# Pair tiles and replicated rows loaded from a DRAM copy of X0, one overlapping transfer each

## What is computed

```python
e = stack([tbl_f[ids[:, f]] for f in range(39)], axis=1)        # (1024, 39, 16)

def cin_layer(X0, Xi, W, b):                                    # H = 128
    Wr = W.reshape(H, 39, Xi.shape[1])
    return einsum('hjk,bjd,bkd->bhd', Wr, X0, Xi) + b[None, :, None]

X0 = e; Xi = X0; res = []
for W, b in ((W0, b0), (W1, b1), (W2, b2)):
    Xi = cin_layer(X0, Xi, W, b)
    res.append(Xi.sum(axis=2))
z = concatenate(res, axis=1)
h = maximum(concatenate([z, dense_ctx], axis=1) @ W_top1 + b_top1, 0)
h = maximum(h @ W_top2 + b_top2, 0)
y = h @ W_top3
```

## Time and profile before

| | us |
|---|---|
| time, median of 3 runs (1387.94 to 1392.07) | 1389.95 |
| the profiled execution's own time | 1388.79 |
| its span | 1386.9 |
| setup, until the first X0 is there | 0 to 56 |
| layer 0 of the first half chunk, TensorE often idle | 56 to 100 |
| one chunk in the steady state (466 to 624) | 158 |
| last MLP steps | 1330 to 1387 |

### The profile page before, as it was taken

How to read it: one execution, slowest core, us unless ns; L and a number is a source line. 1 busy time by engine, 2 the same in 40 slices (tenths; PEclk the granted TensorE clock), 3 DMA queues, 4 the chain that set the end, 5 groups by cost and what they waited for, 6 DMA issues and landing times.

```text
span 1386.9 us, 23238 instructions
## 1 busy us (share of the span) xinstructions
PE 1277.4 (92%) x6029; PEld 1041.8 (75%) x6029; DVE 1082.3 (78%) x2681; ACT 1042.6 (75%) x3356; POOL 893.5 (64%) x663
## 2 busy tenths in 40 slices
PE   3179999999999999999999999999999999999986
PEld 3147777777888787887878777887878788887775
DVE  3068999988877988789877988789877988779940
ACT  2228888878877888788867888688877888688842
POOL 6658676877776687667867597667876266441111
PEclk8559999999999999999999999999999999999998
DMA  6243223413232223303242223313233123310010
GB/s 221 42 115 68 46 72 80 106 30 83 67 97 46 48 63 85 92 21 80 62 108 50 52 63 74 92 33 72 56 90 79 32 68 83 89 32 9 18 39 0
DMA packets 71116, 92.39 MB, mean 67 GB/s; under 512 B 31776, under 2 KB 53792, under 8 KB 69696
## 3 DMA queue, kind: packets, MB, share of 16 engines
q1 hardware_dynamic: 60836, 87.75, 24.4%
q0 software_dynamic: 9984, 2.58, 2.1%
q10 hardware_dynamic: 156, 0.48, 0.1%
HBM read 21.03 MB, written 10.95 MB: 23 GB/s over the span
## 4 chain that ended last, share of the span: by engine, by line
PE 70%; POOL 8%; DVE 7%; issue 6%; DMA 3%; ACT 2%; SPq 2%; ACTq 0%; DVEq 0%; POOLq 0%
PE ring L938 16%; PE ring L940 15%; PE ring L939 15%; PE side L856 5%; POOL e_in L397 4%; PE side L915 4%; PE l_ps L843 4%; PE l_ps L845 3%; PE l_ps L844 3%; DVE terms L785 3%; DVE x_s L741 2%; PE side L871 2%; POOL pairs L429 2%; DMA x_rep<-x_t 2%; POOL pairs_lo L440 2%
## 5 line engine op out<-in xcount | busy, mean ns | idle before, releaser
L626 ACT ACTIVATE terms<-ring,e_both 128x128 f32<-128x128 f32 x2944 | 836.3, 399 | 221.9 <-PE ring L940 219.9
L938 PE MATMUL ring<-w_hi,x_hi 128*128 128x512 f32 (+1 forms) x1280 | 544.8, 426 | 31.4 <-DVE terms L785 27.7
L785 DVE SCALAR_TENSOR_TENSOR terms<-ring,e_both,terms 128x128 f32<-128x128 f32 x1792 | 508.2, 344 | 62.7 <-PE ring L940 58.0
L940 PE MATMUL ring<-w_hi,x_lo 128*128 128x512 f32 (+1 forms) x1280 | 499.7, 390 | 0.0
L939 PE MATMUL ring<-w_lo,x_hi 128*128 128x512 f32 (+1 forms) x1280 | 498.2, 389 | 0.0
L741 DVE TENSOR_REDUCE x_s<-terms 128x32 f32<-128x800 f32 x512 | 488.9, 976 | 0.1
L440 POOL TENSOR_TENSOR pairs_lo<-pairs,pairs_hi 117x1024 fp32r<-117x1024 f32 (+1 forms) x104 | 250.2, 2406 | 191.6 <-ACT pairs_hi L532 190.6
L397 POOL DMA_INDIRECT e_in<-in_tbl,idx x312 | 306.1, 981 | 88.3 <-issue 79.4
L938 PEld LDWEIGHTS ring<-w_hi,x_hi 128*128 128x128 f32 x1280 | 242.8, 190 | 103.0 <-DVE terms L785 42.1
L429 POOL TENSOR_TENSOR pairs<-x_rep,pairs 117x1024 f32<-117x1024 f32 (+1 forms) x104 | 250.3, 2407 | 92.3 <-DMA pairs<-x_t 89.3
L939 PEld LDWEIGHTS ring<-w_lo,x_hi 128*128 128x128 f32 x1280 | 243.4, 190 | 49.2
(11 more groups left out here) (65 smaller groups left out, 610.6 us busy)
## 6 DMA issues: line engine op xcount, KB each, us to landing
pairs<-x_t SPq DMA_DIRECT2D x312, 156.0 KB
x_scratch<-x_s SPq DMA_DIRECT2D x32, 256.0 KB, 2.2
x_r<-x_scratch SPq DMA_DIRECT2D x8, 1024.0 KB, 6.0
x_rep<-x_t SPq DMA_DIRECT2D x45, 156.0 KB
g_t<-in_L_rec_W SPq DMA_DIRECT2D x2, 2496.0 KB, 9.5
e_in<-in_tbl,idx POOLq DMA_INDIRECT x312
x_scratch<-e_both SPq DMA_DIRECT2D x8, 312.0 KB, 7.2
xb<-x_scratch SPq DMA_DIRECT2D x8, 312.0 KB, 3.9
```

The costliest lines, as they stand in the source:

```text
L626: last = nc.scalar.activation(term(d, ACT_BEFORE[d][g] + i), twos(ring[:, (GROUPS * d + g) % RING, i * H:(i + 1) * H]), ACT.Copy, scale=sc ...
L785: nc.vector.scalar_tensor_tensor(out=acc, in0=y, scalar=scale_of(j, d), in1=acc, op0=ALU.mult, op1=ALU.add).then_inc(dve_unit, 1)
L938: nc.tensor.matmul(acc, x1_hi[:, x], w1_hi[:, w], start=True, stop=False)
L940: nc.tensor.matmul(acc, x1_lo[:, x], w1_hi[:, w], start=False, stop=True).then_inc(y_group, 1)
```

## The change

A DRAM tensor `x0t_scratch` of 58 by 2048 is added. A new step on SP's queue, `x0t_write`, copies one half of `x0_t` to it; its semaphore is `x0t_out`. `rep` waits for that copy and loads all 117 rows of `x0_rep` by one transfer whose source has three dimensions: 3 repeats at a step of nothing, 39 rows, 1024 elements. `pair_tile` loads its 117 (or 78) rows by one transfer whose source has 3 (or 2) blocks that begin one row apart and so overlap, 39 rows, 1024 elements. The copy of half 0 stands ahead of `rep`, that of half 1 behind pair tile 1. The first chunk's `rep` moves from ACT's queue to SP's. ACT's evacuation of `x0_t` (line 555) waits for the copies of the chunk before instead of for the loads. Counts on semaphores follow: 16 for each tile instead of 48.

```diff
-                    for n in range(SHIFTS_OF[t]):
-                        s = PER_TILE * t + n
-                        sp.dma_start(products[n * FIELDS:(n + 1) * FIELDS, :],
-                                     x0_t[s:s + FIELDS, half * HALF:(half + 1) * HALF]).then_inc(loaded, 16)
+                    rows = bass.AP(tensor=x0t_dram.tensor, offset=PER_TILE * t * COLS + half * HALF,
+                                   ap=[[COLS, SHIFTS_OF[t]], [COLS, FIELDS], [1, HALF]])
+                    sp.dma_start(products[0:ROWS_OF[t], :], rows).then_inc(loaded, 16)
+
+                def x0t_write(chunk, half):
+                    after(sp, x0t_ready, 4 * chunk + 2 * half + 2)
+                    after(sp, pair_made, PAIR_TILES * (2 * (chunk - 1) + half + 1))
+                    x = slice(half * HALF, (half + 1) * HALF)
+                    sp.dma_start(x0t_dram[:, x], x0_t[:, x]).then_inc(x0t_out, 16)
 
                 def rep(chunk, half):
-                    after(sp, x0t_ready, 4 * chunk + 2 * half + 2)
+                    after(sp, x0t_out, 16 * (2 * chunk + half + 1))
                     after(sp, pair_made, PAIR_TILES * (2 * chunk + half))
-                    for n in range(PER_TILE):
-                        sp.dma_start(x0_rep[n * FIELDS:(n + 1) * FIELDS, :],
-                                     x0_t[0:FIELDS, half * HALF:(half + 1) * HALF]).then_inc(rep_in, 16)
+                    rows = bass.AP(tensor=x0t_dram.tensor, offset=half * HALF,
+                                   ap=[[0, PER_TILE], [COLS, FIELDS], [1, HALF]])
+                    sp.dma_start(x0_rep[:, :], rows).then_inc(rep_in, 16)
...
                 if following:
-                    if layer1:
-                        rep(c + 1, 0)
-                    else:
-                        after(sp, x0t_ready, 2)
+                    x0t_write(c + 1, 0)
+                    rep(c + 1, 0)
                     for i in range(PAIR_TILES):
                         pair_tile(c + 1, i)
+                        if i == X0T_LAST_AFTER:
+                            x0t_write(c + 1, 1)
...
-                            for s in range(2):
-                                if layer1:
-                                    after(act, pair_in[s], loads(c + 1, s))
-                            after(act, rep_in, 16 * PER_TILE * 2 * (c + 1))
+                            after(act, x0t_out, 32 * (c + 1))
...
-                        if following and d == X0T_SLICES[0] + 1:
-                            act.wait_ge(x0t_ready, 2)
-                            for n in range(PER_TILE):
-                                act.dma_start(x0_rep[n * FIELDS:(n + 1) * FIELDS, :],
-                                              x0_t[0:FIELDS, 0:HALF]).then_inc(rep_in, 16)
```

More of the change, by code:

```diff
@@ L32, in build_tower @@
     TILE = [(half, t) for half in range(2) for t in range(PAIR_TILES)]
-    SLOT_BEFORE = [16 * sum(SHIFTS_OF[TILE[k][1]] for k in range(i % 2, i, 2)) for i in range(TILES + 2)]
+    SLOT_BEFORE = [16 * len(range(i % 2, i, 2)) for i in range(TILES + 2)]
     RING = 4
@@ L111, in build_tower @@
     X2_WRITES = {13: 0, 2: 1, 6: 2}
-    X2_LAST_AFTER, X0_AFTER = 9, 11
+    X2_LAST_AFTER, X0_AFTER, X0T_LAST_AFTER = 9, 11, 1
     X2_SLOTS = 8
@@ L185, in pair_slot @@
                 s = i % FIRST_SLOTS
-                count = sum(16 * SHIFTS_OF[k] for k in range(s, i + 1, FIRST_SLOTS))
+                count = 16 * len(range(s, i + 1, FIRST_SLOTS))
                 return pairs[:, s, :] if s < 2 else more_pairs[:, s - 2, :], pair_in[s], count
@@ L189, in pair_slot @@
             return (pairs[:, s, :], pair_in[s],
-                    loads(chunk, s) + SLOT_BEFORE[i] + 16 * SHIFTS_OF[TILE[i][1]])
+                    loads(chunk, s) + SLOT_BEFORE[i] + 16)
         def loads(chunk, s):
-            elsewhere = sum(16 * SHIFTS_OF[i] for i in range(PAIR_TILES) if i % 2 == s and i % FIRST_SLOTS >= 2)
+            elsewhere = 16 * sum(i % 2 == s and i % FIRST_SLOTS >= 2 for i in range(PAIR_TILES))
             return SLOT_BEFORE[TILES + s] * chunk - elsewhere
@@ L198, in build_tower @@
         x0_dram = nc.dram_tensor("x0_scratch", [D, P, FIELDS], f32, kind="Internal").ap()
+        x0t_dram = nc.dram_tensor("x0t_scratch", [WRAPPED, COLS], f32, kind="Internal").ap()
         x2_dram = nc.dram_tensor("x2_scratch", [D, P, H], f32, kind="Internal").ap()
@@ L214, in build_tower @@
         x0t_ps, x0t_ready, x0_out, xb_in = sem("x0t_ps"), sem("x0t_ready"), sem("x0_out"), sem("xb_in")
+        x0t_out = sem("x0t_out")
         rep_in = sem("rep_in")
@@ L392, in _ @@
             sp.wait_ge(x0_out, 16 * CHUNKS)
+            sp.wait_ge(x0t_out, 32 * CHUNKS)
         @block.gpsimd
@@ L426, in multiply_pairs @@
                         pool.wait_ge(pair_made, n)
-                    after(pool, rep_in, 16 * PER_TILE * (2 * chunk + half + 1))
+                    after(pool, rep_in, 16 * (2 * chunk + half + 1))
                     after(pool, loaded, count)
@@ L717, in first_pairs @@
                         if g == made_at:
-                            after(dve, rep_in, 16 * PER_TILE * (2 * chunk + half + 1))
+                            after(dve, rep_in, 16 * (2 * chunk + half + 1))
                             after(dve, loaded, count)
```

## The result

The change makes the kernel slower: median 1572.28 us of 4 runs (1571.42 to 1575.06), against 1389.02 us for the kernel before in runs beside it, a ratio of 1.1315 with a 95% interval of 1.1301 to 1.1329. The forecast was 1549 us, 23 us too little, and inside its range of 1420 to 1690. The profiled execution took 1572.25 us (span 1570.4), 183.5 more than the 1388.79 of before.

A forecast was written before the change was run, and what follows sets the result against it. TensorE, busy 92% of the span, was taken to bound the kernel. 40.3 + 7 x (11.9 + 1.8 + 3.2) = 158.6 us on 1388.79 gave 1547.4, or 1549 us allowing 1.2 to the median; range 1420 to 1690.

The forecast's parts named there:

- the forecast's 7 us: Whole kernel: gain if each coalesced transfer were spread over all DMA engines, giving 1383 us; chance 0.07.
- a busy share of 0.80: Quietest stretch of 39-row loads: read as 13 of 16 DMA engines working, since 13 divides 39.
- copy of 58 rows: Copy of half of `x0_t` to DRAM: two engines, 1.5 us fixed plus 4.7 of data, 6.2 us.
- `x0_rep` and tile 0, one after the other: Two loads after the copy on the same three engines: 8.8 us, then 6.3 more.
- tile 0 late, each chunk: Start of a chunk, seven times: POOL starts at 488.2 instead of 476.31, 11.9 us late with no slack.
- TensorE's waits on ACT, each chunk: TensorE's pauses: 11.9 us at a chunk's start and 3.2 at the change of halves.
- clock, each chunk: Restart after the pause at a chunk's start: 3.6 us at half speed, 1.8 us lost.
- first chunk: Chain of copies and loads without cover: tile 8 at 145.0 instead of 104.71, 40.3 us later.
- The signs that the prediction named: Profile after: first product near 80 us, layer 1 near 140, chunks 175, POOL waiting 18, clock 0.50, DMA share near 3/16.
- The other tiles: Later pair tiles of a half: a load takes 8.8 of the 9.27 us pace, hidden by half a microsecond.
- All wide, 1383: Rival for all transfers: spread in full whatever the outer count, tile 0 2.3 us earlier, 1383 us; chance 0.07.
- Three engines, and slow: Rival for the loads: three engines at 14.4 GB/s make the DMA engine the bound, 1784 us; chance 0.07.

The follow-up runs named there:

- experiment 2: Changed kernel with loads turned to 39 groups of 3 rows, seventh tile padded to 117 rows, copy of 62 rows: 1448.94 us, ratio 1.0428 to the kernel before.
- experiment 5: Changed kernel with one row more in `x0_t` and its copy, 59 instead of 58: 1637.87 us, ratio 1.1777 to the kernel before.
- experiment 3: Changed kernel with loads turned to 39 groups of 3 rows and a copy of 64 rows: 1392.66 us, ratio 1.0031 to the kernel before.
- experiment 4: Changed kernel with each load from DRAM cut into three (two) transfers of 39 rows, copy still 58 rows: 1439.04 us, ratio 1.0358 to the kernel before.

## Why the prediction was right, and by how much it was off

**What decides** was named rightly: a transfer is cut along the outermost counts, three engines for the loads, two for the copies. The trace shows 0.19 (3/16) at 78 GB/s, experiment 2 shows 0.13 (2/16) for a copy of 62 rows, experiment 5 shows 0.06 (1/16), and the steps from 58 to 59 to 64 rows (7.9, 11.8, 3.3 us) are explained neither by size, nor by source, nor by overlap. Single packets agree: the rows of the 58-row copy start in pairs, and in the turned load of experiment 3 thirteen start within 0.2 us of each other. The Trainium skill, "DMA: Bandwidth & Descriptors", section "Why a DMA increments its semaphore by 16 and not by 1", gives this rule, the largest number up to 16 that divides both sides' slowest dimension. It gives 2, 1, 2 and 16 engines for 58, 59, 62 and 64 rows, and the runs agree with each. By the advice of the same page's section "Rules for kernel authors" to coalesce many small transfers, taken alone, the change would have won the forecast's 7 us; another row of the same table warns that an outermost dimension smaller than 16 confines a transfer to at most as many engines, and the runs side with that row: the coalesced form costs 183 us, since the join made 3 the outermost count. Where the join keeps 39 outermost (experiment 2) it wins nothing over three transfers from DRAM (experiment 4): it is 10 us slower, 7 of which are its slower copy.

**The evidence was weaker than its weight.** I had read a busy share of 0.80 as 13/16. That it was near 13/16 was chance, though thirteen engines was right. In experiment 3, where transfers of 39 groups run and everything else but POOL stands, the share is above one:

```profile
65.00:66.00 1.00, 0.00 (x0) 0.00 (x0) 0.00 (x0) 0.00 (x0) 0.69 (x2) 0.50 1.06 313
```

A mean over 16 engines that exceeds 1 adds up packets that overlap or run past the window's end, so with many wide transfers in flight it is no count of engines. Where narrow transfers run with hardly anything beside them, 0.19, 0.13 and 0.06 match 3, 2 and 1 of 16.

**The terms, one by one**, predicted and measured, in us:

| term | predicted | measured |
|---|---|---|
| copy of 58 rows | 6.2 | 7.7 (7.6 in the first chunk) |
| `x0_rep` and tile 0, one after the other | 15.1 | 14.7 |
| tile 0 late, each chunk | 11.9 | 13.1 |
| TensorE's waits on ACT, each chunk | 11.9 + 3.2 = 15.1 | 16.3 |
| waits on DVE and on pair tiles, each chunk | 0 | -0.3 |
| clock, each chunk | 1.8 | 4.3 |
| first chunk | 40.3 | 41.7 |
| sum, first chunk and 7 chunks | 158.6 | 183.5 |

The measured values, but those of the first chunk and the sum, are means of the six chunks. Measured, 41.7 + 7 x 20.2 is 183.1. Cut by time instead, the second chunk's first issue is 43.6 us late, the next six chunks add 121.5, and what follows adds 18.4. Of the 24.9 us that were missing, the clock is 2.5 x 7 = 17.5, the pauses 1.2 x 7 = 8.4, the first chunk 1.4, and the vanished waits take 2 back.

Two terms were mis-sized. **The clock**: the step that failed is the 1.8 us for 3.6 us at half speed, taken once a chunk. A fall costs more, 2.3 to 2.6 us: in the changed kernel TensorE runs on for 5.2 us at the low clock in the mean of the 12 falls. And the clock falls twice a chunk: at the change of halves I charged the pause and not the clock, and the trace shows it fall after 3.90 us as it does after 13.05. Together that is 4.3 us a chunk instead of 1.8. **The copy**: I took 1.5 us of fixed part and 4.7 of data. The packet records show a copy's first row 0.8 us after the issue, its rows moving for 6.3 to 6.8 us, and SP going on 0.3 to 0.6 us behind the last. So the fixed part was not too small; the two engines took a third longer for their 29 rows each (0.20 us a packet in the mean instead of 0.16). The last copy has no gather beside it and still takes 6.3; why stays open. Nor can a copy be priced by rows on an engine and the read rate: with 64 rows the data takes 1.4 us, not 0.6. The longer pauses follow from the copy: 1.5 us longer, with the loads 0.4 shorter, is 1.1 a chunk of the 1.2 measured. In the chunk shown the two pauses are 13.05 and 3.90, 1.8 us over the forecast.

**The signs that the prediction named** came: a first product near 80 (81.44), POOL waiting some 18 us (19.66), clock to 0.50, share 3/16, tiles 6 us apart. Two were off: layer 1 of TensorE begins at 133, not 140, and chunks are 178 us, not 175. For the first I had read that layer 1 can't begin before tile 8; it does in both kernels, at 99.75 against tile 8 at 104.71 before, and at 133.21 against 146.4 now. The other tiles are hidden as said, but barely; POOL waits up to 1.28 us for some in the chunk shown, and over the six chunks TensorE waits 9.8 us for pair tiles (4.9 before), once for 5.1.

**The rivals.** "All wide, 1383" is what experiment 3 builds, and even that is 1392.66: its tile 0 is 0.9 us later, not 2.3 earlier. I had priced the copy at 2.2 us and the two loads together at 4.9; they take 3.3 and 7.0. So the way over DRAM had nothing to win here, even without the narrow transfers. "Three engines, and slow" would need 14.4 GB/s; it was 26. The doubt that the SBUF rate applies fell with it, but only half for the reason given, 13 engines at once between rows of SBUF. SBUF as the source isn't needed: experiment 4 loads 39 rows from DRAM at 197 GB/s with a share of 0.93, 13.2 GB/s per busy engine. The low figure goes with many packets in flight at once.

## What to carry to other kernels

Before you merge small transfers into one, write down the outermost count of both sides: a join that puts 3 in front turned 13 engines into 3, and a few rows more or less (58, 59, 64) changed a copy's time by a factor of up to 3.6. Keep the large count outermost and reorder the consumer's weights, or pad the rows to a multiple of 16 (64 was the one tried). A step that is put in front of a chain without slack is paid for once each time round. A pause that it makes on TensorE can cost 2.3 to 2.6 us of clock on top, whether it lasts 3 us or 13, so count the pauses.

## What the runs showed of the hardware that I had not expected

- Issue time on SP depends on the kind, not only on the number: 39 rows from SBUF to SBUF 0.74 us each, 39 rows from DRAM to SBUF 0.36 (median), 117 rows in three dimensions from DRAM 0.71, turned 0.8, a copy of 58 rows to DRAM 0.22 to 0.3 with nothing queued, of 64 rows 0.5.
- SP is held at an issue where narrow transfers are backed up: the second copy takes 4.83 us to issue in experiment 5, and in the changed kernel a copy up to 5.4 and a tile's load up to 7.6.
- A narrow copy to DRAM is slower per engine than a narrow read from it: 18 GB/s for each of two engines (58 rows in 6.6 us), 23 for one (59 rows in 10.7), against 26.
- The granted clock can fall to 1.2 GHz after a pause of 2.5 us, mostly comes back some 5 us after the restart, and costs about the same for a pause of 4 or of 13 us.
- The mean busy share of the DMA engines can be above 1 (1.06), and is then no measure of how many work.
- DVE's rest of a tile takes 2.4 to 3.2 us beside a product on POOL and 1.25 without one. A gather that POOL issues takes 1.96 instead of 0.95 us where one of DVE's products starts just before it (69.56 behind 69.47, 73.07 behind 73.00 and 76.59 behind 76.51 in the kernel before).
